# Shifted convolution taps held for 64 rows by 576 columns per head, their two halves loaded through two queues and multiplied in two row halves of TensorE

## The reference, cut to what matters

```python
k_f = rfft(kernel, n=2 * L); u_f = rfft(u_masked, n=2 * L)
y = irfft(u_f * k_f, n=2 * L)[..., :L]          # causal convolution of 512 positions with 512 taps
y = (y + u_masked * D[:, None]) * mask[:, None, :]
x = x + y
```

## Time and profile before

| | |
|---|---|
| median of 3 runs | 531.86 us |
| time of the profiled execution | 533.11 us |
| its span, first to last instruction | 531.4 us |
| TensorE busy | 494.7 us |
| VectorE busy | 292.3 us |
| ScalarE busy | 198.0 us |
| GpSimd busy | 46.4 us |
| moved by DMA | 82.74 MB |
| mean granted TensorE clock | 0.997 |

### The profile page before, as it was taken

The page is one execution under the profiler, slowest core; times in us unless marked ns, Lnnn a source line. Parts: engine busy times, 40 slices in busy tenths (PEclk is TensorE's granted clock), DMA queues, the critical chain, the costliest instruction groups (busy, mean ns, idle before and its releaser), DMA issues.

```text
span 531.4 us, 9990 instructions
## 1 busy us (share of the span) xinstructions
PE 494.7 (93%) x2940; PEld 449.0 (84%) x2940; DVE 292.3 (55%) x617; ACT 198.0 (37%) x411; POOL 46.4 (9%) x55
## 2 busy tenths in 40 slices
PE   0098799999999999999999999999999999999997
PEld 0087787989898999999999999898989898989986
DVE  7883176846454555546464547373737474545541
ACT  5791006433333334334342333243434243434330
POOL 1006600100000001000000101010101010101000
PEclk9999899999999999999999999999999999999999
DMA  7899995556555656555555656464646465555520
GB/s 288 267 346 376 331 340 128 122 111 154 116 152 115 144 128 147 126 137 118 142 123 138 130 129 139 108 157 109 157 88 174 101 161 114 153 117 148 110 63 21
DMA packets 175443, 82.74 MB, mean 156 GB/s; under 512 B 128034, under 2 KB 157282, under 8 KB 175426
## 3 DMA queue, kind: packets, MB, share of 16 engines
q1 hardware_dynamic: 175426, 82.54, 60.5%
HBM read 63.46 MB, written 19.04 MB: 155 GB/s over the span
## 4 chain that ended last, share of the span: by engine, by line
PE 88%; DMA 5%; DVE 5%; issue 1%; SPq 0%; ACT 0%; DVEq 0%
PE ps_g L1111 23%; PE ps_u L1111 22%; PE ps_db L1072 13%; PE ps_da L1072 13%; PE ps_x L1064 3%; PE ps_g L1038 3%; DMA toep<-kpad 2%; DMA kpad<-k_sb 2%; PE ps_g L1121 2%; PE ps_u L1122 2%; PE ps_g L1122 2%; PE ps_u L1121 2%; PE ps_u L1038 2%; PE ps_da L1178 1%; PE ps_db L1179 1%
## 5 line engine op out<-in xcount | busy, mean ns | idle before, releaser
L1111 PE MATMUL ps_g<-w_hi,x_hi 128*128 128x512 f32 (+1 forms) x192 | 72.7, 379 | 1.4 <-DVE x_lo L995 1.4
L529 ACT CAST b_spl<-b_raw 64x512 fp32r<-64x512 f32 (+1 forms) x96 | 51.7, 571 | 55.3 <-PE ps_u L1122 35.7
L1111 PE MATMUL ps_u<-w_lo,x_hi 128*128 128x512 f32 (+1 forms) x192 | 71.4, 372 | 0.0
L1111 PE MATMUL ps_u<-w_hi,x_lo 128*128 128x512 f32 (+1 forms) x192 | 71.4, 372 | 0.0
L1111 PE MATMUL ps_g<-w_hi,x_lo 128*128 128x512 f32 (+1 forms) x192 | 71.4, 372 | 0.0
L1111 PE MATMUL ps_u<-w_hi,x_hi 128*128 128x512 f32 (+1 forms) x192 | 71.4, 372 | 0.0
L1111 PE MATMUL ps_g<-w_lo,x_hi 128*128 128x512 f32 (+1 forms) x192 | 70.9, 369 | 0.0
L876 DVE TENSOR_TENSOR b_spl<-b_raw,b_spl 64x512 fp32r<-64x512 f32 (+1 forms) x96 | 57.9, 629 | 15.3 <-ACT b_spl L529 13.7
L933 DVE TENSOR_TENSOR h_act<-h_act,ps_u 128x512 f32<-128x512 f32 (+1 forms) x48 | 30.4, 632 | 58.6 <-PE ps_u L1122 38.9
L1072 PE MATMUL ps_da<-wd_hi,ht_hi 128*128 128x288 f32 (+1 forms) x176 | 52.1, 296 | 0.0
L1072 PE MATMUL ps_da<-wd_lo,ht_hi 128*128 128x288 f32 (+1 forms) x176 | 51.9, 295 | 0.0
(11 more groups left out here) (170 smaller groups left out, 887.7 us busy)
## 6 DMA issues: line engine op xcount, KB each, us to landing
a_raw<-atab SPq DMA_DIRECT2D x64, 152.0 KB, 2.3
toep<-kpad SPq DMA_DIRECT2D x16, 512.0 KB, 7.3
b_raw<-btab SPq DMA_DIRECT2D x128, 64.0 KB, 2.1
h_raw<-hrow SPq DMA_DIRECT2D x30, 256.0 KB, 2.9
um<-xr SPq DMA_DIRECT2D x16, 256.0 KB, 5.4
x<-xT SPq DMA_DIRECT2D x8, 512.0 KB, 6.9
w_raw<-wgu SPq DMA_DIRECT2D x8, 512.0 KB, 9.1
xrow<-x_sq SPq DMA_DIRECT2D x64, 64.0 KB, 2.2
```

The lines of the kernel that those rows point to most:

```text
L529: nc.scalar.copy(b_spl[b_rows(slot), up, 0:w], b_raw[b_rows(slot), up * w:(up + 1) * w]).then_inc(b_hi, 1)
L1111: T.matmul(ps[:, 0:w], xs[:, kb, :], ws[:, kb, col:col + w], start=(kb == 0 and xs is x_hi and ws is w_hi), stop=False)
```

## The change

The Toeplitz tile of a pair no longer has 128 rows and two heads side by side. Head 0 of the pair lies in partitions 0 to 63, head 1 in partitions 64 to 127, and each has 64 shifted rows of 576 columns (512 + 64). The other 64 rows of each 128x128 Toeplitz block are the same rows read 64 columns further left, so `conv` takes two halves of the contraction, each of 64 rows, from the same tile: for each block d, for each half and for each head one matmul of 64 rows by 128 columns, 16 float32 matmuls for a pair in place of 8. The two heads follow each other in the program and use different rows of the array and different PSUM banks. A pair now takes two banks, and there are 3 such double banks (RP = 3) in place of 4 single ones; the third is `ps_x`, half of which holds the adapter mask until `amask_t` is copied, so `conv(2)` waits for that copy.

The rows 0 to 63 are loaded through SyncE's queue as before, the rows 64 to 127 through ScalarE's, which waits for `k_out` and `conv_ps` itself: pairs 0 to 3 after the magnitudes and before trig(1), pairs 4 to 7 between the casts of weights, pairs 8 to 15 after them. VectorE does taps(1) before phases(3). The host lays out `xr` anew; its size is the same.

```diff
@@ constants and tiles @@
+RP = 3
+HR = P // 2
+HW = NL + HR
-            toep = sb(pa, "toep", [P, RC, 2, NL])
+            toep = sb(pa, "toep", [P, RC, HW])
-        ps_g = [top.enter_context(nc.psum_tensor(f"ps_g{i}", [P, 512], F32)) for i in range(2)]
-        ps_u = [top.enter_context(nc.psum_tensor(f"ps_u{i}", [P, 512], F32)) for i in range(2)]
+        ps_c = [top.enter_context(nc.psum_tensor(name, [P, 2, 512], F32)) for name in ("ps_gg", "ps_uu", "ps_xx")]
+        ps_g, ps_u, ps_x = ([both[:, i, :] for i in range(2)] for both in ps_c)
-        ps_c = [ps_g[0], ps_g[1], ps_u[0], ps_u[1]]
@@ sync @@
-        def shifted_taps(pair):
-            return bass.AP(tensor=kpad, offset=pair * (2 * (P + NL)) + 1, ap=[[1, P], [P + NL, 2], [1, NL]])
+        def shifted_taps(pair, h):
+            return bass.AP(tensor=kpad, offset=(2 * pair + h) * (P + NL) + 1, ap=[[1, HR], [1, HW]])
...
-                sp.dma_start(toep[:, slot, :, :], shifted_taps(pair)).then_inc(toep_in[slot], 16)
+                sp.dma_start(toep[0:HR, slot, :], shifted_taps(pair, 0)).then_inc(toep_in[slot], 16)
@@ scalar @@
+            def load_toep(pair):
+                act.wait_ge(k_out[pair // RC], 16)
+                wait(act, conv_ps, pair - RC + 1)
+                act.dma_start(toep[HR:P, pair % RC, :], shifted_taps(pair, 1)).then_inc(toep_in[pair % RC], 16)
             for g in range(1, NG):
                 magnitudes(g)
+            for pair in range(RC):
+                load_toep(pair)
             trig(1)
...
             for n in range(4, NP_GU):
+                if n % 2 == 0:
+                    load_toep(n // 2 + 2)
                 top_part(n)
+            for pair in range(2 * RC, PAIRS):
+                load_toep(pair)
@@ vector @@
-                                  ps_c[pair % RC][:, :].rearrange("p (h n) -> p h n", h=2)).then_inc(x1_ok, 1)
+                                  ps_c[pair % RP][:, :, 0:KB * NB]).then_inc(x1_ok, 1)
...
             tables(1)
+            taps(1)
             phases(3)
-            taps(1)
@@ tensor @@
-                pe.wait_ge(toep_in[slot], 16 * (pair // RC) + 16)
+                pe.wait_ge(toep_in[slot], 32 * (pair // RC) + 32)
                 pe.wait_ge(um_in[slot], 16 * (pair // RC) + 16)
-                wait(pe, x1_ok, pair - RC + 1)
-                for h in range(2):
-                    at = h * KB * NB
-                    for d in range(KB):
-                        v = um[:, slot, h * KB * NB:h * KB * NB + (KB - d) * NB]
-                        last = T.matmul(ps_c[slot][:, at + d * NB:at + KB * NB], toep[:, slot, h, d * P:(d + 1) * P],
-                                        v, start=(d == 0), stop=(d == KB - 1))
+                wait(pe, x1_ok, pair - RP + 1)
+                if pair == RP - 1:
+                    pe.wait_ge(amaskt_ok, 1)
+                for d in range(KB):
+                    for half in range(2):
+                        at = d * P + (1 - half) * HR
+                        for h in range(2):
+                            rows = slice(h * HR, (h + 1) * HR)
+                            v = um[rows, slot, half * KB * NB:half * KB * NB + (KB - d) * NB]
+                            last = T.matmul(ps_c[pair % RP][:, h, d * NB:KB * NB], toep[rows, slot, at:at + P], v,
+                                            start=(d == 0 and half == 0), stop=(d == KB - 1 and half == 1))
@@ host @@
-    xr = xT.reshape(P, NH // 2, 2 * KB * NB)[::-1].transpose(1, 0, 2).reshape(NH // 2 * P, 2 * KB * NB)
+    xr = np.asarray(x).reshape(NB, PAIRS, 2, KB, 2, HR)[..., ::-1].transpose(1, 2, 5, 4, 3, 0)
+    xr = xr.reshape(PAIRS * P, 2 * KB * NB)
```

More of the change, by code:

```diff
@@ L143, in program @@
         ht_lo = sb(top, "ht_lo", [P, FB, P], F32R)
-        ps_g = [top.enter_context(nc.psum_tensor(f"ps_g{i}", [P, 512], F32)) for i in range(2)]
-        ps_u = [top.enter_context(nc.psum_tensor(f"ps_u{i}", [P, 512], F32)) for i in range(2)]
+        ps_c = [top.enter_context(nc.psum_tensor(name, [P, 2, 512], F32)) for name in ("ps_gg", "ps_uu", "ps_xx")]
+        ps_g, ps_u, ps_x = ([both[:, i, :] for i in range(2)] for both in ps_c)
         ps_da = top.enter_context(nc.psum_tensor("ps_da", [P, 512], F32))
         ps_db = top.enter_context(nc.psum_tensor("ps_db", [P, 512], F32))
-        ps_x = [top.enter_context(nc.psum_tensor(f"ps_x{i}", [P, 512], F32)) for i in range(2)]
         ps_k = [ps_da, ps_db]
-        ps_c = [ps_g[0], ps_g[1], ps_u[0], ps_u[1]]
         prm_in, len_in, idx_in = sem("prm_in"), sem("len_in"), sem("idx_in")
@@ L824, in select_conv @@
                     lmask[:, :, b0:b1].unsqueeze(1).broadcast_to([P, 2, KB, b1 - b0]),
-                    ps_c[pair % RC][:, :].rearrange("p (h k b) -> p h k b", h=2, k=KB)[:, :, :, b0:b1])
+                    ps_c[pair % RP][:, :, 0:KB * NB].rearrange("p h (k b) -> p h k b", k=KB)[:, :, :, b0:b1])
             def rem_part(n):
```

## The result

The kernel before took 532.9 us, the changed one 536.64 us (medians of 20 runs each). The ratio is **1.0066, with a 95% interval of 1.0048 to 1.0085**: slower, where 526.0 was forecast, and 0.6 us outside the range. (The forecast started from 531.86, the median of the first three runs; with 20 runs the kernel before is at 532.9, so 5.9 us less were forecast and 3.7 more were measured.) The profiled execution took 537.81 us with a span of 536.0; before it was 533.11 and 531.4.

What follows compares the result with a forecast made beforehand. With fewer bytes, transfers should stop limiting and PE's pace set the end: the convolution ends near 73.1 us instead of 79.0, and 5.9 us off the 531.86 median gives 526.0 us, range 522.5 to 529.5.

Steps and rivals of the forecast that it cites:

- PE's cost of a pair: Convolution matmuls of one pair: 2.41 us as before, the two heads overlapping wholly, weight loads included.
- Weights in a line: Rival, convolution: matmuls overlap but weight loads don't, 3.55 us a pair, 542.3 us in all; chance 0.11.
- part overlap: Rival, convolution: the two heads overlap only in part, some 3.0 us a pair, 533.3 us in all; chance 0.10.
- no overlap: Rival, convolution: nothing of the two heads overlaps, 4.82 us a pair, 564 us in all; chance 0.07.
- the estimate of 3.1 us: Convolution: a pair's cost from the skill page's speedup of 3.07 for four row tiles, 2.41 x 4 / 3.07.
- The 3.05 us a pair: Convolution: the cost of a pair from which weights in a line decides and the gain is zero.
- Steps 1 to 4: Early convolution: conv(0) starts at about 26.8 us, conv(2) at 36.3 behind the mask copy, taps(3) end at 43.2.
- Bytes: Toeplitz tile loads: 3.5 MB less, 9 to 16 us of DMA time, so transfers should stop being the limit.
- Step 5: conv(4) to conv(15): twelve pairs at 2.41 us, 28.9 us together, ending at 72.1 before store waits.
- Step 6: Group 2's tap store: out at 42.3 us, landing in 4 to 6; 1.0 us allowed for pairs 8 and 9.
- the store's queueing stays: Rival, SyncE's queue: x loads ahead keep the 9.13 and 7.68 us waits, middle about 531 us; chance 0.10.
- What was hidden: ScalarE's 16 new load issues, about 0.4 us each, were taken as covered; tables(1) had 0.6 us to spare.

## Why the prediction was wrong

**PE's cost of a pair: right.** 2.41 us, two heads with all their loads side by side (71.48 to 73.89 in the chain). Weights in a line, part overlap and no overlap had 0.28 together; none of them is what happened, and each pair at pace excludes them. The Trainium skill's "TensorE: Matmul & The Clock Gate", Part 3, from which the estimate of 3.1 us was made, is for four row tiles, and its factor doesn't carry over to the two here. The Trainium skill's rule in "TensorEngine Tiling (Array Packing)", Key Properties, agrees with the trace: 32 matmuls and 32 loads in 2.41 us. The 3.05 us a pair at which the prediction put the gain at zero doesn't fit its own sums: at 3.0 us it is already 1.4 us late, so zero lies near 2.9. Nothing hung on it.

**Steps 1 to 4: right to 0.2 us at their end.** conv(0) at 27.39 (26.8 forecast, in its bounds), conv(2) at 36.24 (36.3) behind the mask copy, taps(3) done at 42.98 (43.2). conv(0) and tables(1) were each 0.6 us later than forecast; it didn't show, since its pair took 4.62 us instead of 4.95 and conv(2) waits for the mask copy anyway. Up to here the change costs and gives what was written.

**The step that failed is "Bytes":** "Both are more than PE has idle, so transfers should stop being the limit". It priced 3.5 MB fewer (3.63 by the page) at the rates of before and took the rate as given. The rate belongs to how the transfers are laid out: with halves of 64 partitions it fell from 394 to 265 GB/s (44 to 56 us) and from 328 to 214 (56 to 68), with full engines. Splitting before's own tile that way does the same (249), at 1.0273; for a tile of 64 rows alone, writing them 32 partitions further on undoes it (1.0114 to 0.9921); and with the changed kernel's bytes over 128 partitions the forecast comes true (0.9911, first weight matmul 73.66). So the premise about bytes and the sum over PE were sound, and a fact about the destination was missing. None of the rivals had a falling rate in it: they priced PE and the queue. I had read 217 and 245 GB/s in the earlier trace rows as the rate "while Toeplitz reads are in flight"; they were short stretches, and the 12 us from 44 on, tiles included, had 394.

**Step 5** follows from it. From 43.0 us on, twelve pairs were to take 28.9 us and 1.0 of waits. They took 40.5: the 28.9; 7.38 in four gaps; 1.5 and 1.6 for the two pairs on the slow clock (4.07 and 4.17 against 2.57) and 0.2 for the pair behind; the rest, 0.9, is what a pair ahead of a gap or at the end lasts beyond 2.41 (2.57 to 2.62 from its first start to its last end). The stretch from 56 to 68 has a granted clock of 0.76, between the levels of 1.2 and 2.4 GHz, against 0.86 before: the gaps of 2.04 and 2.86 us there cost 1.5 and 1.6 us more each. I had written that "the slow clock of pair 9 goes with its gap", and there were two instead.

**Step 6** was half right. Group 2's store went out at 41.89 (42.3) but took 7.89 us rather than 4 to 6, and pair 9's tile 11.27. The rival "the store's queueing stays" had priced long times for both (9.13 and 7.68), but mostly by the wrong mechanism: it blamed the x loads ahead in the queue, as did the prediction's first paragraph. Alone on ScalarE's queue, in the kernel before, the store still took 7.0 us of its 9.13.

**What was hidden.** ScalarE's issues were costed at nothing, with "a longer issue would push tables(1)" as the caveat. Each took 0.45 us or more (the first four 0.61) and a table load of 1.28 us that I hadn't counted came behind them, so trig(1) was 1.7 us late and tables(1) waited 0.6. The kernel with both halves on SyncE's queue has none of this and also gets its first tile 1.3 us earlier, and it is on median nearer to before; its interval (1.0004 to 1.0053) just overlaps that of the changed kernel.

## What to carry to other kernels

Before a large transfer is split or shrunk, ask which partitions each piece writes: in these runs pieces for partitions 0 to 63 or 64 to 127 made fewer bytes take longer, and slowed every other transfer in flight; the same piece at 32 to 95 did not. Read the rate (GB/s) beside the engines' share over a long stretch: here a share of 1.07 with the rate down by a third meant that packets had become slower (a median of 84 ns to 126), and the saving in bytes, computed at the old rate, was gone. A gap ahead of a matmul group cost 1.5 us beyond its own 2 to 3 us where the clock fell in it, so a stage just at the edge between transfers and TensorE loses or wins more than its bytes. And follow a gain to the engine that is next in line: with the adapter loads put off, the convolution ended 2.8 us earlier and the kernel was no faster.

## What was not expected of the hardware

- Descriptors of one length take longer while transfers to 64 such partitions are in flight, those of other loads too: in the packet records of 22 to 70 us those of 2048 B had a median of 84 ns before and with rows 32 to 95, 140 with rows 0 to 63, 146 with before's tile in two halves. In the changed kernel, where none of the 2048 B packets belongs to a tile, it was 126.
- Full overlap of two 64-row matmul streams in float32, weight loads included: 32 matmuls and 32 loads in the 2.41 us of 16 and 16.
- A copy from 32 partitions to 32 others (1024 float32 each) takes VectorE 0.69 us, or 1.50 to 2.70 beside GpSimd's subtractions, while GpSimd's own take 2.69 on average instead of 2.37 where VectorE doesn't copy.
- ScalarE's table load isn't moved ahead of DMA issues that stand before its activation: 1.28 us at 24.63 behind four issues, against 19.41, in the shade of a wait, before.
